# Sequence 0 in dense blocks ahead of the sparse ones, in both 8-expert stages of a six-phase kernel

## The reference, cut to what matters

```python
logits = xf @ w_router                       # 8 experts
probs = softmax(logits)
topk_w, topk_idx = top_k(probs, 2)
weights = sum(topk_w[..., None] * one_hot(topk_idx, 8), axis=1)
h = gelu(einsum('te,ieh->tih', xf, w1) + b1) # 128 -> 512, every expert
out = einsum('tih,ihe->tie', h, w2) + b2     # 512 -> 128
out = sum(out * weights[..., None], axis=1)
x = x + 0.5 * out
```

## Time and profile before

| | us |
|---|---|
| median of 3 runs (1598.16 to 1599.77) | 1598.2 |
| the profiled execution | 1597.53 |
| its span in the profile | 1595.8 |
| busy: PE, DVE, ACT, POOL | 1245.3, 1168.6, 854.4, 479.0 |
| POOL scatters (L547), 128 | 131.8 |
| POOL gathers (L272), 128 | 132.1 |
| POOL's copies of expert weights (L915, L920), 92 | 103.9 |

### The profile page before, as it was taken

The page is one execution under the profiler, slowest core; times in us unless marked ns, Lnnn a source line. Parts: engine busy times, 40 slices in busy tenths (PEclk is TensorE's granted clock), DMA queues, the critical chain, the costliest instruction groups (busy, mean ns, idle before and its releaser), DMA issues.

```text
span 1595.8 us, 19797 instructions
## 1 busy us (share of the span) xinstructions
PE 1245.3 (78%) x6193; PEld 726.6 (46%) x6193; DVE 1168.6 (73%) x2508; ACT 854.4 (54%) x1334; POOL 479.0 (30%) x619
## 2 busy tenths in 40 slices
PE   4108998455788879888851999757999888979998
PEld 4107887122222222222211788545666444656665
DVE  5707997359899999999635899657778655668875
ACT  4207776244578867767762877523334366534332
POOL 6763332774000011222137333253451120201000
PEclk9999999677799999999985999969999999989999
DMA  8342221243111111111113222134563111044354
GB/s 269 105 125 73 80 80 67 65 133 109 44 39 32 37 33 43 50 31 31 36 55 103 61 86 80 57 89 88 113 132 78 33 30 31 1 103 85 82 107 107
DMA packets 85909, 119.74 MB, mean 75 GB/s; under 512 B 17829, under 2 KB 39813, under 8 KB 85805
## 3 DMA queue, kind: packets, MB, share of 16 engines
q1 hardware_dynamic: 77612, 101.68, 24.5%
q0 software_dynamic: 8192, 16.79, 3.8%
HBM read 80.13 MB, written 35.39 MB: 72 GB/s over the span
## 4 chain that ended last, share of the span: by engine, by line
PE 56%; DVE 17%; POOL 9%; ACT 7%; issue 7%; DMA 4%; SPq 0%; DVEq 0%; POOLq 0%; ACTq 0%
PE bank L1192 6%; PE bank L1764 6%; POOL xs_rows L547 6%; DVE shared L1704 5%; PE pair L698 5%; PE pair L696 5%; PE pair L697 5%; PE pair L1108 4%; PE pair L1110 4%; PE pair L1109 4%; ACT shared L1754 3%; PE pair L1746 3%; PE pair L1698 3%; POOL staged L272 2%; DVE x_res L285 1%
## 5 line engine op out<-in xcount | busy, mean ns | idle before, releaser
L1704 DVE TENSOR_REDUCE shared<-pair 128x2 f32<-128x1024 f32 x256 | 304.9, 1217 | 24.7 <-PE pair L1698 21.9
L1754 ACT ACTIVATE shared<-pair 128x1024 f32<-128x1024 f32 x256 | 258.7, 1023 | 85.2 <-PE pair L1746 84.9
L742 DVE TENSOR_TENSOR shared<-shared 128x512 fp32r<-128x512 f32 x184 | 175.4, 954 | 30.7 <-ACT shared L732 27.5
L1159 ACT ACTIVATE shared<-pair 128x512 f32<-128x512 f32 x144 | 85.7, 595 | 184.5 <-PE pair L1110 184.5
L547 POOL DMA_INDIRECT xs_rows<-shared,slots x128 | 131.8, 1030 | 134.1 <-ACT shared L1754 80.9
L1108 PE MATMUL pair<-shared 128*128 128x512 f32 x288 | 157.9, 548 | 0.2 <-DVE shared L1118 0.2
L696 PE MATMUL pair<-shared 128*128 128x512 f32 x368 | 152.8, 415 | 0.0
L1764 PE MATMUL bank<-shared 128*9 128x512 f32 x1024 | 143.9, 636 | 8.8 <-ACT shared L1754 8.8
L272 POOL DMA_INDIRECT staged<-ys_rows,slots x128 | 132.1, 1032 | 61.6 <-issue 36.5
L726 ACT ACTIVATE shared<-pair,shared 128x512 f32<-128x512 f32 x184 | 126.7, 691 | 43.6 <-PE pair L698 37.8
L698 PE MATMUL pair<-shared 128*128 128x512 f32 x368 | 145.8, 396 | 0.0
(11 more groups left out here) (319 smaller groups left out, 2289.5 us busy)
## 6 DMA issues: line engine op xcount, KB each, us to landing
shared<-p_coef_rows SPq DMA_DIRECT2D x64, 512.0 KB, 8.5
shared<-xs_rows SPq DMA_DIRECT2D x46, 256.0 KB, 2.8
ys_rows<-shared SPq DMA_DIRECT2D x46, 256.0 KB, 2.0
xs_rows<-shared SPq DMA_DIRECT2D x1, 5888.0 KB, 22.6
staged<-in_L_ffn_w SPq DMA_DIRECT2D x16, 256.0 KB, 4.7
shared<-in_L_ffn_w SPq DMA_DIRECT2D x16, 256.0 KB, 3.2
p_q_parts<-shared SPq DMA_DIRECT2D x8, 384.0 KB, 2.8
p_k_parts<-shared SPq DMA_DIRECT2D x8, 384.0 KB, 3.2
```

Of the source, the lines that this page charges most:

```text
L1704: nc.vector.tensor_reduce(mneg[:, i, 2 * c:2 * c + 2], pair_of("max", b, m)[:], AX_X, ALU.max, negate=True).then_inc(s["mx_read"], 1)
L1754: nc.scalar.activation(probs[st % 2][:, 2 * p:2 * p + 2, :], pair_of("exp", b, 2 * st + p)[:], ACT.Exp, scale=scale).then_inc(s["exp_done" ...
```

## The change

Sequence 0 leaves the sparse path. In both 8-expert stages its 512 tokens go through all eight experts in eight dense blocks (i < D = 8) that stand ahead of the sparse ones; NBLK becomes (2 x 7 x 512 + 8 x 511) / 512 = 21, so there are 29 blocks for 23.

- A dense block reads x of sequence 0 (transposed and split once), takes the weights from w_all without POOL's copy and the biases from vecs, and its y_dve adds the result times w_dense (the routing weight of that expert, zero if it was not chosen) to x_res. The cast of the high part is ACT's in all four units. There is no combine and no gather for sequence 0.
- The eight dense blocks stand where the scatters are made; POOL's scatters of the last groups are paced by units of the dense blocks (beside). Weight splitting, the tables and the routing weights are put between units.
- First stage: routing order 1 to 7, then 0 (ORDER); the weights of experts 0 and 1 are split ahead of sequence 5. The x transpose of the first sparse block is put behind block 7 (X_LATE).
- Second stage: the routing of sequence 7 and of group (7) lies between the dense units; POOL makes the low weight parts of experts 4 to 7 (w_lo_pool) between its scatters, so DVE makes four.
- The norm of sequence 0 for the next phase is done inside the sparse blocks (first_norm_pe and so on), so the next phase starts with it ready. POOL gathers sequence 1 right after the last store; its combine in attention comes after the first split of k.
- Attention routes three groups (1, 2), (3, 4), (5, 6) instead of four, and sends half a group in each of the sequences 4 to 7.

```diff
-NBLK = (2 * B * T + NE0 * (T - 1)) // T
+NBLK = (2 * (B - 1) * T + NE0 * (T - 1)) // T
+ALL = NE0 + NBLK
...
-        GROUPS = (((0, 2), (2, 5), (5, 8)), ((0, 2), (2, 4), (4, 6), (6, 7), (7, 8)))
+        ORDER = ((1, 2, 3, 4, 5, 6, 7, 0), tuple(range(B)))
+        GROUPS = (((1, 3), (3, 6), (6, 8)), ((1, 3), (3, 5), (5, 7), (7, 8)))
...
+            def w_lo_pool(g, e):
+                g.wait_ge(s["w_hi"], NE0 * occ + e + 1)
+                nc.gpsimd.tensor_tensor(w_parts[:, e, :, 1, :], w_stage[e % 4], w_parts[:, e, :, 0, :], ALU.subtract).then_inc(s["w_lo_pool"], 1)
...
+                    if dense(i) and occ and i > 3:
+                        nc.tensor.wait_ge(s["w_lo_pool"], i - 3)
+                    elif dense(i):
+                        nc.tensor.wait_ge(s["w_lo"], NE0 * occ + i + 1)
...
+                w = w_all[:, i * 4 * HID:i * 4 * HID + 2 * HID] if dense(i) else w_up[(i - D) % 2]
...
             def y_dve(v, i):
-                v.wait_ge(s["yback"], NBLK * occ + i + 1)
+                v.wait_ge(s["yback"], ALL * occ + i + 1)
+                if dense(i):
+                    if i:
+                        v.wait_ge(s["dve_done"], dve_no("y", i - 1))
+                    for k in range(TILES):
+                        last = nc.vector.scalar_tensor_tensor(out=x_res[:, k, :], in0=bank[7][:, k * P:(k + 1) * P], scalar=w_dense[:, k, i:i + 1],
+                                                              in1=x_res[:, k, :], op0=ALU.mult, op1=ALU.add)
...
                     group_copy(occ, 0, bank[4])
+                    w_hi_act(0)
+                    w_hi_act(1)
+                    for k in range(4, 7):
...
+            def beside(g, k, ahead):
+                if k > ahead:
+                    g.wait_ge(s["up_ready"], U0 + min(k - ahead, HC * D))
...
-                    group_send(g, occ, 2)
+                    group_send(g, occ, 2, pace=lambda k, m: beside(g, k * 7 // 4, 1))
                 else:
                     seq_root(g, occ, B - 1)
-                    group_send(g, occ, 2, 1, 2)
-                    group_send(g, occ, 3)
-                    group_send(g, occ, 4)
+                    group_send(g, occ, 2, pace=lambda k, m: beside(g, k * 3 // 4, 2))
+                    w_lo_pool(g, 4)
+                    w_lo_pool(g, 5)
+                    group_send(g, occ, 3, pace=lambda k, m: beside(g, 12 + k, 2))
+                    w_lo_pool(g, 6)
+                    w_lo_pool(g, 7)
...
                 y_wait(g, occ)
-                if n + 1 < len(phases):
-                    gather(g, occ, 0)
-                    gather(g, occ, 1, FIRST_HALF)
-                    norm_b(base(n + 1))
+                gather(g, occ, 1)
...
-            GROUP_STEPS = ((2, late), (4, late), (6, late), (7, last_body))
+            GROUP_STEPS = ((3, late), (5, late), (7, last_body))
```

More of the change, by code:

```diff
@@ L425, in seq_R @@
             for i in range(TILES):
-                last = nc.tensor.matmul(to[:, i * NE0:(i + 1) * NE0], xnT[b % 2][:, i * P:(i + 1) * P], wr0[:], start=True, stop=True)
+                last = nc.tensor.matmul(to[:, i * NE0:(i + 1) * NE0], xnT[ORDER[occ].index(b) % 2][:, i * P:(i + 1) * P], wr0[:], start=True, stop=True)
             last.then_inc(rs_["pe_step"], 1)
@@ L640, in tables_dve, with dense, prep @@
                 nc.vector.tensor_scalar(onehot[:], ex_all[0:NE0, :], row_no[:], None, ALU.is_equal).then_inc(s["dve_step"], 1)
[L643 to L649 removed]
+            def dense(i):
+                return i < D
+            def prep(i):
+                return 0 if dense(i) else i - D + 1
+            PREPS = NBLK + 1
             per_ld = [len(range(k, NBLK, 3)) for k in range(3)]
@@ L683, in moe0_phase, with xT_dense, xT_pe @@
             U0 = UNITS * occ
+            def xT_dense():
+                for k in range(TILES):
+                    last = nc.tensor.transpose(bank[6][:, k * P:(k + 1) * P], xn_rows[occ][:, k, :], ident[:])
+                last.then_inc(s["xT_ps"], 1)
+            def xT_pe(i):
+                j = i - D
+                nc.tensor.wait_ge(s[f"x_ld{j % 3}"], 16 * (per_ld[j % 3] * occ + j // 3 + 1))
+                nc.tensor.wait_ge(s["dve_done"], dve_no("xl", prep(i) - 1))
+                if i == D:
+                    nc.tensor.wait_ge(s["act_step"], act_at(occ, "bias"))
+                if i == NORM + 2:
+                    nc.tensor.wait_ge(xnT_ready, base(n + 1) + 1)
+                for k in range(TILES):
+                    last = nc.tensor.transpose(bank[6][:, k * P:(k + 1) * P], xb[j % 3][:, k * E:(k + 1) * E], ident[:])
+                last.then_inc(s["xT_ps"], 1)
@@ L693, in xl_dve, with first_norm_pe @@
-                nc.vector.tensor_tensor(xl[i % 2][:], bank[6][:], xh[i % 2][:], ALU.subtract).then_inc(s["dve_done"], 1)
+                q = prep(i)
+                v.wait_ge(s["act_done"], act_no("xh", q))
+                nc.vector.tensor_tensor(xl[q % 2][:], bank[6][:], xh[q % 2][:], ALU.subtract).then_inc(s["dve_done"], 1)
+            NORM = D + 8
+            def first_norm_pe(f):
+                nc.tensor.wait_ge(xn_ready, f + 1)
+                nc.tensor.wait_ge(s["dve_done"], dve_no("xl", prep(NORM + 1)))
+                for i in range(TILES):
+                    last = nc.tensor.transpose(bank[6][:, i * P:(i + 1) * P], xn[:, i, :], ident[:])
+                last.then_inc(xnT_ps, 1)
@@ L799, in tensor @@
+                for i in range(ALL):
+                    if D < i + 1 < ALL or i + 1 == D and not X_LATE:
                         xT_pe(i + 1)
@@ L845, in scalar @@
-                w_hi_act(2)
-                w_hi_act(3)
-                weights_act(occ)
-                bias_act()
-                for e in range(4, NE0):
-                    w_hi_act(e)
-                xh_act(0)
-                for i in range(NBLK):
-                    if i + 1 < NBLK:
+                    xh_act(0)
+                c_.wait_ge(vecs_ready, 1)
+                for i in range(ALL):
+                    if D < i + 1 < ALL or i + 1 == D and not X_LATE:
                         xh_act(i + 1)
```

502 lines of the change are left out of this document (314 added, 188 removed).

## The result

The changed kernel takes 1571.15 us (median of four runs, 1570.08 to 1576.10) against 1598.99 beside it (1598.16 to 1601.48): ratio 0.983, 95% interval 0.9805 to 0.9854. It is faster, by 28 us where 58 were forecast, and 0.15 us outside the range of 1523 to 1571. The profiled execution took 1570.53 us, its span 1568.8.

What follows compares the result with a forecast made beforehand. It took TensorE to bound the expert blocks, waiting around them for routing, GpSimd's scatters and gathers. Terms of -22.9, -12.7, -5, -1.3 and -16.1 sum to -58.0 us, from 1598.2 to 1540 us; range 1523 to 1571.

Steps and rivals of the forecast that it cites:

- first dense matmul, first stage: Start of the first stage's dense blocks: at 60.7 us, after early weight casts, a shorter last group and a tile split.
- first sparse matmul: First stage, behind dense blocks and scatters: at 115.5 us where it was 123.73, a step of -8.2 us.
- sparse half, first stage: 21 sparse blocks for 23 (-12.8), start-up paid earlier (-2.5), next phase's first transposes put in (+0.6).
- hand-over to attention: First stage to attention: sequence 0 needs no gather, so later sequences come one round sooner, -12.7 us.
- attention's second half: Attention routes three groups instead of four: -5 us, taken between 1 and 9.2.
- second stage: Second 8-expert stage: later first sparse matmul (+13.4), fewer blocks (-12.8), start-up (-2.5), transposes (+0.6): -1.3 us.
- into the 16-expert stage: Sequence 0's work runs beside sequence 1's gather, whose combine comes 15.6 us after the last copy, not 31.7: -16.1 us.
- B: Rival: scatters starve beside the dense blocks, each waiting for a gap of VectorE; +216 us, 1756 us; chance 0.04.
- C: Rival: TensorE's clock stays at the lower level through both dense halves; +86 us, 1626 us; chance 0.03.
- A: Rival: gather rounds not won in full (half of 12.7 + 16.1 lost), dense halves stall 10 us; 1564 us; chance 0.21.
- I take 60 us from x to the first sparse matmul (56 to 68): Second stage's dense half: 60 us from complete x to first sparse matmul, where it was 46.7; +13.4 us.
- The -2.5 for the start-up: Sparse halves of both 8-expert stages: lower clock, ScalarE's table and two x splits already paid in the dense half; -2.5 us.

Runs made afterwards that it cites:

- e7: Changed kernel with two of VectorE's first-stage weight subtractions parted by the routing weights: 1575.51 us, ratio 0.9886 to the kernel before.
- e9: Changed kernel with GpSimd writing zeros instead of its four low-part subtractions in the second stage: 1582.17 us, ratio 0.9855 to the kernel before.
- e1: Changed kernel with GpSimd's four second-stage low parts made by VectorE: 1565.88 us, ratio 0.979 to the kernel before.
- e4: Changed kernel with only sequence 0's second-stage routing weights ahead of the first sum, the rest at unit (7,0): 1570.47 us, ratio 0.9836.
- e5: Changed kernel, second stage: dense choice and sequence 0's weights made at the start, other weights in three pieces behind the first sum: 1566.45 us, ratio 0.9783.
- e12: Changed kernel, second stage: choice and sequence 0's weights early, all low parts on VectorE, last sequence's routing and ScalarE's casts of experts 4 to 7 later: 1582.08 us.
- e2: Changed kernel with each of GpSimd's second-stage low parts made twice: 1580.4 us, ratio 0.9904 to the kernel before.
- a0: The changed kernel again, unedited, on a second chip: 1590.24 us, ratio 0.9909 to the kernel before.

## Why the prediction was wrong

Each term, forecast and measured. The end of the first stage is taken at its last matmul (by its last copy the sparse half is 0.4 us longer and the hand-over as much shorter):

```
                                        forecast   measured
first dense matmul, first stage           60.7       59.5
first sparse matmul                       -8.2       -7.0
sparse half, first stage                 -14.7       -7.7
hand-over to attention                   -12.7      -11.8
attention's second half                   -5.0       -3.1
second stage                              -1.3      +20.7
into the 16-expert stage                 -16.1      -15.9
rest of the kernel                         0         -2.2
sum                                      -58.0      -27.0
```

**Right.** The start of the first dense half, its length (112 forecast for the blocks' end; TensorE was done with them at 112.3), the scatters as its bound (TensorE then waited 1.5 and 1.9 us for the rows that they wrote; by e7 the dense blocks are the next bound, 1 us below), their spacing beside the blocks (1.56 us from 60.19 to 108.64, the row of 4.92 among them, for 1.46), both hand-overs, and GpSimd's subtraction (2.5 forecast, 2.36 measured). Rivals B and C did not occur; the clock in the dense halves was 1.00 and 0.82. Of A, the lost gather rounds did not occur (27.7 of 28.8 us won), and the stalls did, in one stage, with 16 us for the 10 put there. Of all the numbers given, A's 1564 is nearest to the measured time, by its stalls alone.

The Trainium skill (SBUF — State Buffer, Who interferes with whom) says that a VectorE instruction with two SBUF inputs contends with a GpSimd instruction that reads SBUF, "not with one that only writes it". The changed kernel and e9 agree: 5.83 us beside the subtractions, 0.67 beside the zeros. Its inference that such instructions don't stall descriptor generation does not fit the scatter of 4.92 us, nor its fall to 2.59 in e7.

**The step that failed: "I take 60 us from x to the first sparse matmul (56 to 68)".** It was 76.0 (800.86 to 876.82 us), 16 of the 22 us missed in that stage. The prediction added up each engine's list (GpSimd 50, ScalarE 52, TensorE 46) and took the longest, with "bubbles about 4". The lists were about right, or too long: of the 66 us from 804 to 870 TensorE was busy 48.5, VectorE 48.6, ScalarE 43.3, GpSimd 38.7. What was missed is that in this stage one chain runs through the engines in turn while they do the dense blocks: the last sequence's normalisation and copy on ScalarE, its router on TensorE, the choice on VectorE, positions on TensorE, slots, tables and weights on VectorE, and behind them all in VectorE's queue the first weighted sum, for which TensorE waits. Each station stands in a queue that is in use. In the first stage the routing was nearly done when the blocks began, and the same estimate held. The experiments show it: an edit at one place alone gave 0.3 to 3.1 us at the end of the stage (e1, e4, e5, e9), and edits at the queues of all four engines in turn gave 10.6 (e12); the first sparse matmul then comes 65.4 us behind x, within the range that was given. Where the 5 us above the 60 go was not looked for.

**"What VectorE loses to GpSimd's reads is covered by TensorE being six units ahead"** put a term at nothing that lay on this chain. TensorE's lead is no cover, since it ends at a bank that VectorE empties. Taking the first lock (5.1 us) away brought the sum 2.9 us forward with 2.4 us of work added to VectorE (e1), and some 5 us more of it put the sum 3.9 us back (e2). It is a part: with both locks gone and their work on VectorE, 3.1 of the 16 us were won. e9, meant to price the lock alone, is spoilt by ScalarE's stop.

**The -2.5 for the start-up** had the wrong sign. In the kernel before, the first sparse blocks were the quick ones: gelu to gelu 3.89, 5.94 and 5.99 us, since there are no down matmuls yet for six units. In the changed kernel the first sparse block takes 7.70 (first stage), with both kinds of matmuls and two x splits. From the first sparse matmul to the last one the stages are 7.7 and 8.6 us shorter, not the 12.8 of two blocks: 5.1 and 4.2 us are lost again. Of these 1.27 are the next phase's transposes (a block of 7.66 for 6.39), forecast as 0.6, and the other 3.8 and 3.0 the start-up, forecast as a gain of 2.5. These make up 7 us in the first stage and 6 in the second.

By the traces' milestones, the first stage and its hand-over bring 26.6 us, and the second with its hand-over loses 5 (+20.7 - 15.9): its dense blocks cost more than the gather they save. Dense blocks in the first stage alone, some 5 us better by this count, were not tried.

## What to carry to other kernels

When work is moved beside other work, don't compare the lengths of the engines' lists: follow the one chain that passes through all of them, count its stations, and give each the queue that it stands in. What is emptied last by a shared bank or buffer sets how far the engine ahead can run. To price a lock, take it away and add up what the queue gained and what was put into it instead, as in e1; and before one profile is compared with another, look in both for an engine that stands still with its inputs ready, or its stop is taken for the effect of the edit, as here in e9.

## What the runs showed of the hardware

- A VectorE subtraction of two SBUF operands is held for the whole of two GpSimd subtractions of 128x1024 (5.83 us for 0.69), and is not held by GpSimd's writes of the same size (0.67; 0.98 us each).
- An indirect scatter that takes 0.96 us took 4.92 beside a row of such subtractions without a gap, and 2.59 when the row was cut short (e7).
- ScalarE stood still for 10.7 us, or for 23.6 in four stops, with nothing to wait for in the profile, on two of four chips and in every profile there (seven), at one place or more between 50 and 95 us; and for 3.1 and 3.9 us some 25 us into the second dense half in two of the four profiles of one of these chips (e9, a0). The cause is open. On these two chips the change was worth 14 and 15 us, on the first 28.
- The same code ran with 10.24 us at half clock in one profile and without it in the next (three of the eight profiles of new kernels on the first chip), at a cost of 4 us (the block beside it 10.7 for 6.5).
